# Attention's rough scores: one 128-row contraction against three 64-row matmuls in the two halves of TensorE's array

## The chip, the cores and the metric

The kernel is one launch on one NeuronCore of a Trainium2 chip. The metric is device time in microseconds (us) of one execution. TensorE (PE in the rows) multiplies, its weight loads are recorded apart (PEld); VectorE is DVE, ScalarE is ACT, GpSimd is POOL. In a matmul the stationary operand is loaded into the array and the moving operand's columns stream past it; both lie on SBUF partitions, and the partitions are the rows of the array over which the contraction runs.

## The reference, cut to what matters

The model normalizes 1250 rows of 768 features, sends them through two graph attention layers, and then through a transformer layer: attention with 12 heads of width 64, and a mixture of 8 experts. The change touches the attention's scores alone:

```python
def _attention(x, Wqkv, Wproj):                     # x: [1, 1250, 768], H = 12, HD = 64
    qkv = (x @ Wqkv).reshape(B, T, 3, H, HD)
    q, k, v = (qkv[:, :, 0], qkv[:, :, 1], qkv[:, :, 2])
    scores = jnp.einsum('bqhd,bkhd->bhqk', q, k) * jnp.float32(HD) ** (-0.5)
    attn = jax.nn.softmax(scores, axis=-1)
    out = jnp.einsum('bhqk,bkhd->bqhd', attn, v).reshape(B, T, D)
    return out @ Wproj
```

The softmax needs for each query a number near the maximum of its scores, to be subtracted before the exponential. It cancels in the quotient, so it need not be exact.

## The kernel before, in words

All matmuls of the attention take float32r operands. Precision is kept by splitting: a rounded part ("hi") and what it lacks ("lo").

Two heads make a pair `p` (six pairs), `e` is 0 or 1 within it. For each head four tiles of 128 partitions and 1250 columns hold, with `r = 64 * e`:

- `qst[:, e]`: q_hi in rows `r` to `r+63`, q_lo in the other half. `split` steps 0 and 2 on DVE write them (L1057, L1063) from `raw`.
- `kst[:, e]`: k_hi in both halves. DVE writes half `r` (L1060, `split` step 1), ACT writes the other (`set_k`, L946).
- `q2[:, e]`: a copy of q_hi in half `r` (`set_q` on ACT, L951), and in the first row of the other half the negated maxima (`set_m` on ACT, L956 and L957).
- `k2[:, e]`: k_lo in half `r` (`split` step 3 on DVE, L1067), and a row of ones in the first row of the other half (POOL, L1533 and L1534).

So `kst` times `qst` (L843) gives k_hi q_hi + k_hi q_lo, and `k2` times `q2` (L845) adds k_lo q_hi and the maxima's row. Both contract over 128 rows.

Before a head's scores can be taken, its maxima are needed. `rough(p, e, t)` (L811) computes the scores of 125 queries against all 1250 keys as three matmuls over the full 128 rows, 512, 512 and 226 columns, into PSUM banks 0 to 2 (L822 to L824). `maximum` on DVE (L1072) reduces those 1250 columns to one column, and the next `rough` waits for it, since there is one set of three banks. After ten of them `maxima` (L832) turns the ten columns into a row, and `set_m` writes it into `q2`.

The order of work is written out by hand. A head has 25 units `j`. In each unit TensorE takes four score matmuls of 250 columns (`scores`, L843 and L845) and six matmuls of 250 columns for an earlier unit (`weighted`, L864 to L866), ACT takes two exponentials of 500 columns (L974, L976), and DVE or POOL subtracts them (L1035, two and three units in five). Into this the next head's preparation is put by unit numbers: `ROUGH_AT[e]` gives the units after which TensorE takes a `rough` and before which DVE takes a `maximum`; `SET_K_AT`, `SET_Q_AT` and `SET_M_AT` give the units after which ACT writes `kst`, `q2` and the maxima. In head (p, 0) the preparation of (p, 1) is done, in head (p, 1) that of (p+1, 0). Between the two heads `project` (L793) computes q and k of the next pair, 108 matmuls of 416 or 418 columns, and ACT evicts them into `raw` (L939).

The first head's roughs stand before the pairs, between halves of the value projection (L912 to L915, `v_half`), with `set_q(0, 0)` on ACT after one more eviction of values (L1019, L1020). Each engine takes its instructions in the order in which they are written. Of the tuples above the first number belongs to the preparation of e = 1 and the second to that of e = 0.

Of the kernel before, what the change touches and what calls it, by code (L numbers as in the profile page):

```python
# [6 lines left out]
N = 1250  # L7
P = 125
# [95 lines left out]
def build(nc, x, src, dst, gw1, gas1, gad1, gb1, gw2, gas2, gad2, gb2,  # L104
# [123 lines left out]
    qst = put("qst", [128, 2, N], f32r, at=HEADS)  # L228
# [94 lines left out]
    with ctx:  # L323
# [3 lines left out]
        def sem(name):  # L327
            if name not in sems:
                sems[name] = ctx.enter_context(nc.semaphore(name))
            return sems[name]  # L330
# [435 lines left out]
        NUM_AT = ((8, 13, 18, 22), (9, 13, 18, 22))  # L766
        O_HI_AT, O_LO_AT = (18, 21), (20, 24)
        LAST_AT = ((10, 14, 20), (1, 5))
        SPLIT_AT, SET_K_AT, SET_Q_AT, SPLIT_QK_AT, LOWER_QK_AT = 2, (0, 3), 7, 9, (12, 14)

        def place(e, j):

# [16 lines left out]
        def attention_pe(pe):  # L789
# [21 lines left out]
            def rough(p, e, t):  # L811

                if t == 0:
                    pe.wait_ge(sem("q_lo"), 2 * p + e + 1)
                    pe.wait_ge(sem("k_hi"), 2 * p + e + 1)
                    pe.wait_ge(sem("kst_set"), 2 * p + e + 1)
                    pe.wait_ge(sem("raw_set"), 6 * p + 6)
                    if e == 1:
                        pe.wait_ge(sem("m_set"), 4 * p + 2)
                else:  # L820
                    pe.wait_ge(sem("max"), 20 * p + 10 * e + t)
                for c, (a, b) in enumerate(((0, 512), (512, 1024), (1024, N))):  # L822
                    last = pe.matmul(bank(c, P, b - a), qst[:, e, t * P:(t + 1) * P],  # L823
                                     kst[:, e, a:b], start=True, stop=True)  # L824
                last.then_inc(sem("rough"), 1)

            def maxima(p, e):
# [94 lines left out]
        def attention_act(act):  # L922
            def split_qk(p):
                act.wait_ge(sem("wq_in"), 32 * p + 32)

                if not isinstance(p, int) or p > 0:
                    act.wait_ge(sem("qk_raw"), 6 * p)
                act.activation(wqhi[:, :, :, :].rearrange("p m k c -> p (m k c)"),
                               wqst[:, :, :, :].rearrange("p m k c -> p (m k c)"), ACT.Copy).then_inc(sem("wq_hi"), 1)

            def set_raw(p, chunks=range(6)):

                if (not isinstance(p, int) or p > 0) and chunks[0] == 0:
                    act.wait_ge(sem("qk_split"), 2 * p)
                for j in chunks:
                    m, c = j // 3, j % 3
                    at, n = CHUNKS[c]
                    act.wait_ge(sem("qk_raw"), 6 * p + (j + 1))
                    act.activation(raw[:, m, at:at + n], bank(c, 128, n), ACT.Copy).then_inc(sem("raw_set"), 1)  # L939

            def set_k(p, e):

                r = 64 * e
                act.wait_ge(sem("raw_set"), 6 * p + 6)
                act.wait_ge(sem("q_hi"), 2 * p + e + 1)
                act.activation(kst[64 - r:128 - r, e, :], raw[r:r + 64, 1, :], ACT.Copy).then_inc(sem("kst_set"), 1)  # L946

            def set_q(p, e):

                r = 64 * e  # L950
                act.activation(q2[r:r + 64, e, :], qst[r:r + 64, e, :].bitcast(f32), ACT.Copy).then_inc(sem("q2_set"), 1)  # L951

            def set_m(p, e):
                r = 64 * (1 - e)
                act.wait_ge(sem("m_raw"), 2 * p + e + 1)
                act.activation(halves(q2[r:r + 1, e, 0:1000]), two(0, 1, 500), ACT.Copy).then_inc(sem("m_set"), 1)  # L956
                act.activation(q2[r:r + 1, e, 1000:N], bank(2, 1, 250), ACT.Copy).then_inc(sem("m_set"), 1)  # L957

            def numerators(p, e, g):

                act.wait_ge(sem("pv"), PAIR * p + (UNITS * e + 5 * g + 5 + PV0))
                if e == g == 0:
                    act.wait_ge(sem("v_set"), 2 * p + 2)
                b = (6 + (NG * e + g) % 2) * BANK
                act.activation(outt[64 * e:64 * e + HD, ds(p, 1), g * GQ:(g + 1) * GQ].rearrange("c o q -> c (o q)"),
                               ps[0:HD, b:b + GQ], ACT.Copy).then_inc(sem("o_part"), 1)

            def exps(p, e, between):

                for j in range(UNITS):  # L970
                    n = UNITS * e + j
                    act.wait_ge(sem("st"), PAIR * p + (n + 1))
                    act.wait_ge(sem("pv"), PAIR * p + (n + 1 + PV0 - RING))
                    act.activation(prhi[:, n % RING, :], bank(3 + n % 3, P, 2 * GQ), ACT.Exp, scale=float(HD) ** -0.5)  # L974
                    wait_lo(act, p, e, j - place(e, j)[1])
                    act.activation(prob[:, n % 3, :], bank(3 + n % 3, P, 2 * GQ), ACT.Exp, scale=float(HD) ** -0.5)\  # L976
                        .then_inc(sem("exp"), 1)
                    if j in between:
                        between[j]()

            def pair(p, last):
                steps = {SET_K_AT[0]: lambda: set_k(p, 1), SET_Q_AT: lambda: set_q(p, 1), SET_M_AT[0]: lambda: set_m(p, 1)}
                more = {}
                if not last:
                    steps[SPLIT_QK_AT] = lambda: split_qk(p + 1)
                    more = {LAG - 1: lambda: set_raw(p + 1, (5,)), SET_K_AT[1]: lambda: set_k(p + 1, 0),
                            SET_Q_AT: lambda: set_q(p + 1, 0), SET_M_AT[1]: lambda: set_m(p + 1, 0)}
                else:
                    for k in range(KD):
                        (steps, more)[k // 3][5 * (k % 3) + 9] = lambda k=k: split_act(act, 3, wpst, wphi, (k,))  # L990
                for g, j in enumerate(NUM_AT[0]):
                    steps[j] = lambda g=g: numerators(p, 0, g)
                if not isinstance(p, int) or p > 0:
                    steps[4] = lambda: numerators(p - 1, 1, NG - 1)
                exps(p, 0, steps)
                if not last:
                    for g, j in enumerate(NUM_AT[1]):
                        more[j] = lambda g=g: numerators(p, 1, g)
                    set_raw(p + 1, (0,))
                    numerators(p, 0, NG - 1)  # L1000
                    set_raw(p + 1, range(1, 5))
                else:
                    more[4] = lambda: numerators(p, 0, NG - 1)
                    for t in range(2):
                        more[O_HI_AT[t]] = lambda t=t: o_hi(act, t)
                exps(p, 1, more)

            act.sem_inc(sem("exp"), 3)
            act.sem_inc(sem("o_part"), 2)
            for t in range(T // 2 - 1):  # L1010
                if t:
                    v_higher(act, 2 * t + 2)
                v_higher(act, 2 * t + 3)
                v_out(act, t)
                if t == 1:
                    split_qk(0)
            set_raw(0)
            set_k(0, 0)
            v_out(act, T // 2 - 1)  # L1019
            set_q(0, 0)  # L1020
            for t in range(T // 2, T):
                v_out(act, t)
            set_m(0, 0)
            pair(0, False)
            with act.Fori(0, H // 2 - 2) as i:
                pair(i + 1, False)
            pair(H // 2 - 1, True)
# [16 lines left out]
        def attention_dve(dve, order):  # L1044
# [4 lines left out]
            def split(p, e, step):  # L1049
# [8 lines left out]
                elif step == 1:  # L1058
                    dve.wait_ge(sem("raw_set"), 6 * p + 6)
                    dve.tensor_copy(kst[r:r + 64, e, :], raw[r:r + 64, 1, :]).then_inc(sem("k_hi"), 1)  # L1060
                elif step == 2:
                    dve.wait_ge(sem("q_hi"), 2 * p + e + 1)
                    dve.tensor_tensor(qst[64 - r:128 - r, e, :], raw[r:r + 64, 0, :], qst[r:r + 64, e, :].bitcast(f32),  # L1063
                                      ALU.subtract).then_inc(sem("q_lo"), 1)
                else:
                    dve.wait_ge(sem("k_hi"), 2 * p + e + 1)
                    dve.tensor_tensor(k2[r:r + 64, e, :], raw[r:r + 64, 1, :], kst[r:r + 64, e, :].bitcast(f32),  # L1067
                                      ALU.subtract).then_inc(sem("qk_split"), 1)

            def maximum(p, e, t):  # L1070
# [402 lines left out]
        def _(pool):  # L1473
# [56 lines left out]
            pool.wait_ge(sem("v_row"), T)  # L1530
            order.did(pool.memset(k2[:, :, :].bitcast(f32), 0.0))
            order.wait()
            order.did(pool.memset(k2[64:65, 0, :].bitcast(f32), 1.0))  # L1533
            order.did(pool.memset(k2[0:1, 1, :].bitcast(f32), 1.0))  # L1534
            order.wait()
            pool.sem_inc(sem("set_pool"), 1)
            pool.wait_ge(sem("tile_y"), 3 * T + 2)
# [983 lines left out]
```

## Time and profile before

| | |
|---|---|
| time, median of 3 runs | 1533.46 us (1529.39 to 1536.1) |
| span of the profiled execution, first to last instruction | 1528.7 us |
| mean granted TensorE clock | 0.970 of 2.4 GHz |
| TensorE busy, matmuls | 1412.6 us (92%), 8981 |
| TensorE busy, weight loads | 1337.2 us (87%), 8981 |
| VectorE busy | 1154.8 us (76%) |
| ScalarE busy | 970.2 us (63%) |
| GpSimd busy | 493.7 us (32%) |
| rough matmuls (L823) | 360, from 598.8 to 1164.2 us |

The profile is one execution. The median of the runs is 4.8 us above its span; that is what lies around the span, and the spread between the runs. A busy share counts a matmul from its start to the modelled end of its results; such intervals overlap, so the time that a matmul costs TensorE is read from the start of one to the start of the next.

### The profile page before, as it was taken

The numbers are of one execution on the slowest core, as the hardware profiler recorded it, in microseconds if no ns is written. First come the engines' busy times: TensorE is split into PE (matmuls) and PEld (weight loads), VectorE is DVE, ScalarE is ACT, GpSimd is POOL, SyncE is SP. The second block draws the span as 40 slices with busy tenths as digits, with TensorE's granted clock in tenths as the row PEclk, the third lists the DMA queues.
The fourth block names the chain that finished last, engine by engine and source line by source line (L and its number), as shares of the span: only waits on it lengthen the run. The fifth ranks groups of instructions, "written<-read, shape, count | busy, mean of one in ns | idle before, by whom it ended". The sixth has DMA issues, their size and how long they took to land.

```text
span 1528.7 us, 25668 instructions
## 1 busy us (share of the span) xinstructions
PE 1412.6 (92%) x8981; PEld 1337.2 (87%) x8981; DVE 1154.8 (76%) x1756; ACT 970.2 (63%) x1658; POOL 493.7 (32%) x366
## 2 busy tenths in 40 slices
PE   3898799999799999999999999999999998699996
PEld 1897577999699999899898998999988898599996
DVE  6788979735689762486877868778788787888885
ACT  7997787522368431366848767478587522599995
POOL 2000000000000010244625536256356501288886
PEclk9999799999899999999999999999999998799999
DMA  7001000122214540000000000000001496476752
GB/s 202 1 1 36 6 14 18 52 100 73 102 54 131 182 142 22 1 21 1 1 21 0 21 0 0 21 0 0 21 1 32 121 296 165 126 155 162 164 94 36
DMA packets 52312, 99.09 MB, mean 65 GB/s; under 512 B 10848, under 2 KB 26852, under 8 KB 52224
## 3 DMA queue, kind: packets, MB, share of 16 engines
q1 hardware_dynamic: 40848, 75.68, 15.9%
q0 software_dynamic: 11376, 22.29, 7.5%
q8 instruction: 49, 0.80, 0.2%
q14 instruction: 39, 0.32, 0.1%
HBM read 67.15 MB, written 44.31 MB: 73 GB/s over the span
## 4 chain that ended last, share of the span: by engine, by line
PE 68%; DVE 9%; issue 3%; DMA 1%; ACT 1%; POOL 1%; POOLq 0%; ACTq 0%; DVEq 0%; SPq 0%
PE ps L372 14%; PE ps L373 14%; PE ps L374 14%; PE ps L823 4%; PE ps L864 4%; PE ps L843 3%; PE ps L866 3%; PE ps L845 3%; PE ps L865 3%; DVE mcol L1072 2%; PE ps L1257 1%; PE ps L598 1%; DVE prlo L1035 1%; PE ps L832 1%; PE ps L1674 1%
## 5 line engine op out<-in xcount | busy, mean ns | idle before, releaser
L1035 POOL TENSOR_TENSOR prlo<-prob,prhi 125x500 fp32r<-125x500 f32 x180 | 251.8, 1404 | 267.9 <-ACT prob L976 266.9
L1072 DVE TENSOR_REDUCE mcol<-ps 125x1 f32<-125x1250 f32 x120 | 174.9, 1458 | 73.0 <-PE ps L823 72.5
L974 ACT ACTIVATE prhi<-ps 125x500 fp32r<-125x500 f32 x300 | 176.8, 589 | 71.4 <-PE ps L845 65.4
L864 PE MATMUL ps<-prhi,vhi 125*128 125x250 f32 x600 | 172.5, 287 | 8.0 <-POOL prlo L1035 3.8
L976 ACT ACTIVATE prob<-ps 125x500 f32<-125x500 f32 x300 | 176.4, 588 | 0.6 <-DVE prlo L1035 0.6
L1529 POOL MEMSET q<- 128x2500 f32 x1 | 2.2, 2187 | 528.4 <-PE ps L374 528.4
L866 PE MATMUL ps<-prlo,vhi 125*128 125x250 f32 x600 | 168.8, 281 | 0.0
L865 PE MATMUL ps<-prhi,vlo 125*64 125x250 f32 x600 | 167.8, 280 | 0.0
L1674 PE MATMUL ps<-ohs,ohd 128*125 128x417 bf16 x380 | 126.0, 384 | 39.9 <-DVE ohs L2110 37.1
L843 PE MATMUL ps<-qst,kst 128*125 128x250 f32 x600 | 156.3, 284 | 3.5 <-ACT q L957 1.4
L372 PE MATMUL ps<-hhi,pthi 125*125 125x384 f32 x400 | 153.7, 384 | 3.0 <-DVE ptlo L712 3.0
L845 PE MATMUL ps<-q,k 128*125 128x250 f32 x600 | 153.5, 280 | 0.0
L1035 DVE TENSOR_TENSOR prlo<-prob,prhi 125x500 fp32r<-125x500 f32 x120 | 108.9, 908 | 46.3 <-ACT prob L976 45.3
L373 PE MATMUL ps<-hhi,ptlo 125*125 125x384 f32 x400 | 136.6, 341 | 0.0
L374 PE MATMUL ps<-hlo,pthi 125*125 125x384 f32 x400 | 135.9, 340 | 0.0
L864 PEld LDWEIGHTS ps<-prhi,vhi 125*128 125x128 f32 x600 | 114.4, 191 | 13.9 <-issue 5.5
L2110 DVE TENSOR_SCALAR ohs<-iota,scol,sval 128x420 bf16<-128x420 f16 x380 | 124.3, 385 | 0.0
L843 PEld LDWEIGHTS ps<-qst,kst 128*125 128x125 f32 x600 | 112.5, 188 | 10.6 <-issue 3.8
L1802 ACT ACTIVATE ohd<-iota,drel 128x125 bf16<-128x125 f16 x380 | 119.5, 390 | 0.3 <-POOLq L1502 0.3
L866 PEld LDWEIGHTS ps<-prlo,vhi 125*128 125x128 f32 x600 | 114.2, 190 | 0.0
L845 PEld LDWEIGHTS ps<-q,k 128*125 128x125 f32 x600 | 113.0, 188 | 0.0
L1674 PEld LDWEIGHTS ps<-ohs,ohd 128*125 128x125 bf16 x380 | 54.3, 144 | 65.8 <-DVE ohs L2110 47.2
(330 smaller groups left out, 4026.9 us busy)
## 6 DMA issues: line engine op xcount, KB each, us to landing
w1all<-in_L_ffn_W_dram SPq DMA_DIRECT2D x8, 1152.0 KB, 8.4
w2st<-in_L_ffn_W_dram SPq DMA_DIRECT2D x8, 1152.0 KB, 6.4
wqst<-in_L_ffn_Wqkv_dram SPq DMA_DIRECT2D x12, 384.0 KB, 4.2
hid_d<-tin SPq DMA_DIRECT2D x10, 375.0 KB
hin<-hid_d SPq DMA_DIRECT2D x10, 375.0 KB
vtin<-xn_d SPq DMA_DIRECT2D x10, 375.0 KB
out_dram<-accr POOLq DMA_DIRECT2D x10, 375.0 KB, 8.4
xall<-in_x_dram SPq DMA_DIRECT2D x5, 672.0 KB
```

Of the source, the lines that this page charges most:

```text
L372: pe.matmul(o, lhi, rhi, start=start, stop=False)
L373: pe.matmul(o, llo, rhi, start=False, stop=False)
L374: return pe.matmul(o, lhi, rlo, start=False, stop=stop)
L843: pe.matmul(o, kst[:, e, kt * P:(kt + 1) * P], qst[:, e, g * GQ:(g + 1) * GQ], start=True, stop=False)
L845: last = pe.matmul(o, k2[:, e, kt * P:(kt + 1) * P], q2[:, e, g * GQ:(g + 1) * GQ], start=False, stop=True)
L864: pe.matmul(ps[:, b:b + GQ], vhi[:, e, kt, :], hi, start=kt == 0, stop=False)
L865: pe.matmul(ps[0:HD, b:b + GQ], vlo[:, e, kt, :], hi, start=False, stop=False)
L866: last = pe.matmul(ps[:, b:b + GQ], vhi[:, e, kt, :], lo, start=False, stop=kt == T - 1)
L974: act.activation(prhi[:, n % RING, :], bank(3 + n % 3, P, 2 * GQ), ACT.Exp, scale=float(HD) ** -0.5)
L1035: eng.tensor_tensor(prlo[:, n % RING, :], prob[:, n % 3, :], prhi[:, n % RING, :].bitcast(f32), ALU.subtract)\
L1072: dve.tensor_reduce(mcol[:, e, t:t + 1], ps[0:P, 0:N], AX.X, ALU.max, negate=True).then_inc(sem("max"), 1)
L1674: pe.matmul(into, hots(b)[:, i, :], ohs[:, g % OHS, 0:PACK], start=u == 0, stop=u == WINDOW - 1).then_inc(sem("oh_free"), 1)
```

## The change

`rough` multiplies q_hi and k_hi alone, over 64 rows. Its three matmuls take different halves of the array: columns 0 to 511 and 1024 to 1249 in the half in which `qst` holds q_hi, columns 512 to 1023 in the other half, where `kst` holds its second k_hi. For that the copy of q_hi in `q2` moves to the other half, and with it k_lo in `k2`; the maxima's row and the ones change to the half left free. `rough` waits for q_hi and for the copy (`q2_set`) and no longer for q_lo. `set_q` waits for `q_hi` and is called after unit 1 or 4 where it was after unit 7; for the first head it is called one eviction earlier.

```diff
-        SPLIT_AT, SET_K_AT, SET_Q_AT, SPLIT_QK_AT, LOWER_QK_AT = 2, (0, 3), 7, 9, (12, 14)
+        SPLIT_AT, SET_K_AT, SET_Q_AT, SPLIT_QK_AT, LOWER_QK_AT = 2, (0, 3), (1, 4), 9, (12, 14)
+        ROUGH_PARTS = ((0, 0, 512), (1, 512, 1024), (0, 1024, N))
@@ rough
-                    pe.wait_ge(sem("q_lo"), 2 * p + e + 1)
+                    pe.wait_ge(sem("q_hi"), 2 * p + e + 1)
+                    pe.wait_ge(sem("q2_set"), 2 * p + e + 1)
@@
-                for c, (a, b) in enumerate(((0, 512), (512, 1024), (1024, N))):
-                    last = pe.matmul(bank(c, P, b - a), qst[:, e, t * P:(t + 1) * P],
-                                     kst[:, e, a:b], start=True, stop=True)
+                for other, a, b in ROUGH_PARTS:
+                    r = 64 * (1 - e if other else e)
+                    last = pe.matmul(ps[0:P, a:b], (q2 if other else qst)[r:r + 64, e, t * P:(t + 1) * P],
+                                     kst[r:r + 64, e, a:b], start=True, stop=True)
@@ set_q
-                act.activation(q2[r:r + 64, e, :], qst[r:r + 64, e, :].bitcast(f32), ACT.Copy).then_inc(sem("q2_set"), 1)
+                act.wait_ge(sem("q_hi"), 2 * p + e + 1)
+                act.activation(q2[64 - r:128 - r, e, :], qst[r:r + 64, e, :].bitcast(f32), ACT.Copy).then_inc(sem("q2_set"), 1)
@@ set_m
-                r = 64 * (1 - e)
+                r = 64 * e
@@ pair (ACT)
-                steps = {SET_K_AT[0]: lambda: set_k(p, 1), SET_Q_AT: lambda: set_q(p, 1), SET_M_AT[0]: lambda: set_m(p, 1)}
+                steps = {SET_K_AT[0]: lambda: set_k(p, 1), SET_Q_AT[0]: lambda: set_q(p, 1), SET_M_AT[0]: lambda: set_m(p, 1)}
@@
-                            SET_Q_AT: lambda: set_q(p + 1, 0), SET_M_AT[1]: lambda: set_m(p + 1, 0)}
+                            SET_Q_AT[1]: lambda: set_q(p + 1, 0), SET_M_AT[1]: lambda: set_m(p + 1, 0)}
@@ before the first pair (ACT)
             set_k(0, 0)
+            set_q(0, 0)
             v_out(act, T // 2 - 1)
-            set_q(0, 0)
@@ split, step 3
-                    dve.tensor_tensor(k2[r:r + 64, e, :], raw[r:r + 64, 1, :], kst[r:r + 64, e, :].bitcast(f32),
+                    dve.tensor_tensor(k2[64 - r:128 - r, e, :], raw[r:r + 64, 1, :], kst[r:r + 64, e, :].bitcast(f32),
@@ POOL
-            order.did(pool.memset(k2[64:65, 0, :].bitcast(f32), 1.0))
-            order.did(pool.memset(k2[0:1, 1, :].bitcast(f32), 1.0))
+            order.did(pool.memset(k2[0:1, 0, :].bitcast(f32), 1.0))
+            order.did(pool.memset(k2[64:65, 1, :].bitcast(f32), 1.0))
```

## Rows read from the trace of the kernel before

**Rows 1.** The page: each engine's busy time, and the chain's engines.
```profile
PE 1412.6 (92%) x8981; PEld 1337.2 (87%) x8981; DVE 1154.8 (76%) x1756; ACT 970.2 (63%) x1658; POOL 493.7 (32%) x366
...
PE 68%; DVE 9%; issue 3%; DMA 1%; ACT 1%; POOL 1%; POOLq 0%; ACTq 0%; DVEq 0%; SPq 0%
```

**Rows 2.** Timeline of PE (start us, us, engine, line): end of project, four units, one rough.
```profile
699.83 0.35 PE L374 MATMUL ps<-xtlo,wqhi 128*128 128x416 f32 x1
...
702.11 0.35 PE L374 MATMUL ps<-xtlo,wqhi 128*128 128x416 f32 x1
702.30 0.28 PE L843 MATMUL ps<-qst,kst 128*125 128x250 f32 x1
...
706.73 0.28 PE L865 MATMUL ps<-prhi,vlo 125*64 125x250 f32 x1
706.85 0.28 PE L866 MATMUL ps<-prlo,vhi 125*128 125x250 f32 x1
706.97 0.73 PE L823 MATMUL ps<-kst,qst 128*125 128x512 f32 x3
707.54 0.29 PE L843 MATMUL ps<-qst,kst 128*125 128x250 f32 x1
```

**Rows 3.** Timeline of PE at 1227 us: matmuls of 16 and 8 columns, back to back.
```profile
1227.07 0.25 PE L1225 MATMUL ps<-wrhl,ythi 128*125 128x16 f32 x1
...
1228.05 0.25 PE L1226 MATMUL ps<-wrhl,ytlo 128*125 128x8 f32 x1
```

**Rows 4.** Timeline at 709 us, PE and its weight loads: a restart after a wait.
```profile
709.08 0.27 PE L845 MATMUL ps<-q,k 128*125 128x250 f32 x1
...
709.28 0.19 PEld L864 LDWEIGHTS ps<-prhi,vhi 125*128 125x128 f32 x1
...
709.50 0.28 PE L865 MATMUL ps<-prhi,vlo 125*64 125x250 f32 x1
```

**Rows 5.** Timeline of ACT, head (1, 1): set_k, exponentials, and set_q.
```profile
801.71 1.25 ACT L946 ACTIVATE kst<-raw 64x1250 fp32r<-64x1250 f32 x1
...
803.47 0.58 ACT L976 ACTIVATE prob<-ps 125x500 f32<-125x500 f32 x1
...
807.08 1.25 ACT L951 ACTIVATE q<-qst 64x1250 fp32r<-64x1250 f32 x1
```

**Rows 6.** Timeline of PE, same head: its first rough.
```profile
804.54 0.73 PE L823 MATMUL ps<-kst,qst 128*125 128x512 f32 x3
```

**Rows 7.** Timeline of DVE, head (1, 0): maxima and what stands between them.
```profile
750.40 1.45 DVE L1072 TENSOR_REDUCE mcol<-ps 125x1 f32<-125x1250 f32 x1
...
761.64 1.57 DVE L1040 TENSOR_TENSOR wqlo<-wqst,wqhi 128x768 fp32r<-128x768 f32 x1
763.25 1.46 DVE L1072 TENSOR_REDUCE mcol<-ps 125x1 f32<-125x1250 f32 x1
```

**Rows 8.** Timeline of PE, same head: two of its roughs.
```profile
752.23 0.75 PE L823 MATMUL ps<-kst,qst 128*125 128x512 f32 x3
...
764.76 0.85 PE L823 MATMUL ps<-kst,qst 128*125 128x512 f32 x3 [0.35 <-DVE mcol L1072]
```

**Rows 9.** Busy time by engine: heads (1, 0) and (5, 0).
```profile
core 0: us, PE busy (x) PEld busy (x) DVE busy (x) ACT busy (x) POOL busy (x), PEclk, DMA share, GB/s
...
737.40:774.00 36.60, 35.45 (x274) 33.51 (x275) 31.84 (x28) 30.34 (x58) 24.85 (x17) 1.00 0.08 22
...
1130.00:1167.00 37.00, 33.86 (x258) 31.49 (x257) 35.70 (x32) 29.39 (x57) 28.66 (x20) 1.00 0.08 23
```

**Rows 10.** Timeline of all engines at the first rough, before the pairs.
```profile
596.38 1.25 ACT L946 ACTIVATE kst<-raw 64x1250 fp32r<-64x1250 f32 x1
...
597.22 1.46 DVE L1063 TENSOR_TENSOR qst<-raw,qst 64x1250 fp32r<-64x1250 f32 x1
598.71 1.45 DVE L1067 TENSOR_TENSOR k<-raw,kst 64x1250 fp32r<-64x1250 f32 x1
...
598.78 0.78 PE L823 MATMUL ps<-kst,qst 128*125 128x512 f32 x3
```

## The prediction

> **What bounds the kernel now.** I read the page first: TensorE is busy for 92% of the span, and 68% of the chain that ended last is TensorE's own [rows 1]. A busy share says little for matmuls that overlap, so I went on to the timeline of one head of attention and read the distance from one start to the next [rows 2]. From 699.83 to 702.11 there are 12 matmuls of 416 columns, 0.190 us each. From 702.30 to 706.97 there are 40 matmuls of 250 columns, 0.117 us each. Nothing stands between them: TensorE has work from start to start and is the bound here, at the full granted clock (1.00, 2.4 GHz) [rows 9]. Between the two sizes lie 0.073 us for 166 columns, 0.44 ns a column, which leaves 0.007 us for the matmul itself. A rough takes from 706.97 to 707.54, 0.57 us [rows 2]. The same two figures give it 0.232 + 0.232 + 0.107 = 0.571, for 512, 512 and 226 columns. So the price of columns is well known, and 120 roughs cost TensorE 68 us.
>
> Then the busy time by engine, to see who comes next. In head (1, 0) DVE is busy for 31.8 of 36.6 us, in the last pair's head (5, 0) for 35.7 of 37.0 [rows 9]. DVE takes each rough's maximum, and the next rough waits for it. In (5, 0) DVE and not TensorE sets the pace.
>
> **The change, part by part.** *The rough itself.* Let the first matmul (A, 512 columns) start at 0 in one half of the array. The second (B, 512, other half) has weights of its own to load. What a load of 125 columns costs when nothing hides it I take from matmuls with so few columns that only their loads are left: nine intervals from 1227.07 to 1228.05, 0.109 us each [rows 3]. B starts at 0.11 and its columns end at 0.34. The third (C, 226) needs A's half: from 0.232 to 0.339. Its weights load beside A and B. The next full matmul starts at 0.34 where it started at 0.571. So a rough gives back one matmul of 512 columns, 0.232 us, and 120 of them 27.8 us. This holds if the halves run beside each other and the array changes between one tile and two for nothing; no row here shows a 64-row matmul, so the cost of a rough is bounded from both sides: 0.34 at best, 0.57 if the halves take turns, and above that if changing over costs something (priced below). I take 0.34.
>
> What speaks for the free change is the nearest row. L865 has a stationary operand of 64 columns, 125*64, between two of 128. It starts 0.12 after L864 and 0.12 before L866, as all others do [rows 2], and there are 600 of these. A matmul that uses half the array's columns between matmuls that use all costs nothing. It is the other dimension, so it is a hint and no proof.
>
> The Trainium skill (TensorEngine Tiling (Array Packing), Key Properties) says that changing the tiling mode, not just the tile, drains the engine. If the 64-column matmul is such a mode, this case's rows disagree for columns, 0.12 us on either side; no run here yet shows rows. The Trainium skill (TensorE: Matmul & The Clock Gate, Part 3) says that matmuls in different row groups run at the same time; by that the sum is as above, by the first rule it is the rival below.
>
> *The copy of q_hi, earlier.* The rough now waits for `set_q`, 1.25 us on ACT [rows 5], where it waited for q_lo. q_lo was no gain to lose: inside the pairs DVE writes k_hi after it, and the rough still waits for k_hi.
> In heads (p, 1) the copy now stands behind the exponentials of unit 4. In head (1, 1) these end at 803.47 + 0.58 = 804.05, so the copy ends at about 805.35, and the rough that started at 804.54 [rows 6] starts at about 805.4, 0.85 late. Queued behind it on TensorE are the scores and weighted sums of units 7 and on, which wait too. ACT's exponentials 5 to 7 come 1.25 us later, and where the copy was (807.08) they have caught up. Short waits of TensorE for exponentials and their differences in the units behind it swallow some of that, I assume 0.15: 0.7 a pair, 3.5 us for five. The bounds are 0 (other stalls swallow it) and 1.25, 0 to 6 us in all.
> In heads (p, 0) the copy stands behind unit 1 and the rough behind unit 3. Two units of ten matmuls, 2.3 us, lie between, and the copy takes 1.25; exponential 2 comes 1.25 us later, which TensorE's lead of three units over its use covers. I take 0; without that cover it would be up to 1.25 a head.
> Before the pairs, `set_k` ends at 597.63 and the copy at about 598.9, where the rough started at 598.78 [rows 10]: 0.15 us once. The eviction behind it has two matmul groups of slack.
>
> *Where DVE takes back what TensorE gives.* In head (1, 0) the rough of 752.23 follows a maximum that ended at 751.85, 0.38 us before [rows 7, 8]. Three roughs gain 0.70 by then, so 0.3 is lost. The rough of 764.76 waits for a maximum that started at 763.25, behind `wqlo` (1.57 us): there DVE is in arrears since the rough two before, and one more 0.23 is lost. Together 0.55 a head in five heads, 2.8 us. In (5, 0) DVE has 1.3 us of idle left [rows 9]; I give it 1.0 of the 2.3. Elsewhere, as where two roughs stand in adjacent units, the wait for the maximum moves with the rough, which ends earlier itself, and nothing is lost.
>
> *Edits with one answer.* k_lo now crosses halves as q_lo did: 1.46 us crossing, 1.45 not [rows 10]. The copy crosses as `set_k` does, 1.25 both [rows 5]. The maxima's row and the ones are one partition each in either half. Adding q_lo k_hi no longer to the rough changes a number that cancels in the quotient. No DMA is moved.
>
> **The sum**, against the profiled span of 1528.7 us. Before the pairs 2.3 - 0.15 = 2.2. Heads (p, 0), five: 5 x (2.32 - 0.55) = 8.9. Heads (p, 1), five: 5 x (2.32 - 0.7) = 8.1. Head (5, 0): 1.0. Together 20.2 us, which gives a span of 1508.5. The median of the runs is 4.8 above the span, so 1513.
>
> **Rivals.**
> 1. *Changing over costs more than the columns give back.* Two changes a rough: into halves and out of them. If each waits until the results before it are out, it adds 0.28 - 0.117 = 0.163 us [rows 2]. If the weights can only be loaded after that, the load is no longer hidden: in a restart the load starts at 709.28 and the second next matmul at 709.50, 0.22 where 0.117 is the rule, 0.10 more [rows 4]. So 0.33 to 0.53 a rough against 0.232: 0.09 to 0.30 lost, 11 to 36 us, and the copy's 3.7 on top: 1548 to 1573. It decides from 0.085 us a change, since 20.2 / 120 = 0.17 is what two may cost. For it: the rule above. Against it: the 600 matmuls of L865. If this is so, the starts of L823 and of the L843 behind it are far apart.
> 2. *The halves take turns.* Then a rough costs 0.57 as before, and the copy's 3.7 us are all that is left: 1537. For it: nothing in this trace runs two matmuls at once. It is also how the change would fail to do what it says.
> 3. *Half a gain.* C starts only when B is done, 0.109 + 0.232 + 0.107 = 0.448 a rough: 0.123 x 120 = 14.8, less 3.7, less some 1 for DVE: 10 us, 1523. Or the halves run as hoped and DVE's arrears take all of the heads (p, 0): 1513 + 9 = 1522. For it: DVE's 87% in (1, 0). Against: its idle time there stands right before maxima, where it waits for the rough.
>
> **How the numbers follow.** The forecast 0.55, the third rival 0.15, the second 0.13, the first 0.17. A difference of over 0.5%, 7.7 us, is what a measurement of this kernel can tell from none. Faster by more: 0.55 and three quarters of 0.15, 0.66. Slower by more: the first rival less a little for small prices, 0.16. The rest 0.18. The range goes from 1504, all 27.8 us with a low run, to 1541, the turn-taking with the copy's dearer bound; it leaves out the first rival.
>
> **What would show it.** In the profile after, a rough's first start and the next L843's stand 0.34 us apart and B's start lies 0.11 behind A's (right), 0.57 (second rival), 0.45 with C late (third), or over 0.6 (first). The first rough of each head (p, 1) waits for ACT's copy by some 0.8 us, those of the heads (p, 0) don't. Waits for `mcol` grow in heads (p, 0) by half a microsecond each. The forecast is wrong if the spacing of roughs to their neighbours is off, since all else together is 8 us.

## The result, and the profile after

The changed kernel takes 1545.9 us (median of 4 runs, 1541.5 to 1547.4) against 1532.8 in the same comparison: ratio 1.0076, 95% interval 1.0058 to 1.0093. It is slower by 0.8%, where 1513 was forecast. The ratios of the experiments below are taken against runs of the kernel before made beside them (medians 1534.0 to 1534.5 us); one of those, at 2793.6 us, is left out of them.

| | before | after |
|---|---|---|
| span of the profiled execution | 1528.7 us | 1545.7 us |
| TensorE busy, matmuls | 1412.6 us (92%) | 1423.1 us (92%) |
| weight loads | 1337.2 us (87%) | 1317.3 us (85%) |
| VectorE busy | 1154.8 us (76%) | 1147.3 us (74%) |
| from the value projection to the last maxima | 639.0 us | 650.6 us |
| from there to the end | 361.9 us | 367.7 us |

The page of the changed kernel, busy times and the chain's engines, which answer to [rows 1]:

```profile
PE 1423.1 (92%) x8981; PEld 1317.3 (85%) x8981; DVE 1147.3 (74%) x1756; ACT 971.7 (63%) x1658; POOL 502.9 (33%) x366
...
PE 66%; DVE 6%; issue 4%; POOL 3%; ACT 2%; DMA 2%; ACTq 0%; POOLq 0%; SPq 0%; DVEq 0%
```

TensorE's loads are busy 20 us less and its matmuls 10.5 us more, though the change takes work away from it. 11.6 us of the 17 lie in the attention. I don't put the 5.8 behind it down to the change: the stretch from the last maxima to the end took 361.9 and 365.9 us in two traces of the kernel before, and between 362.0 and 368.5 in the twelve others, in no order that follows the edits (362.0 in `twice`, which has the most 64-row matmuls, and 368.5 in before_spread, which has none).

To see one rough, I take the stretch before the pairs, where it stands between matmuls of the value projection and waits for nothing. First the kernel before, timeline of PE:

```profile
621.09 0.34 PE L374 MATMUL ps<-wvlo,xthi 128*125 128x384 f32 x1
621.27 0.76 PE L823 MATMUL ps<-kst,qst 128*125 128x512 f32 x3
621.87 0.35 PE L372 MATMUL ps<-wvhi,xthi 128*125 128x384 f32 x1
622.05 0.33 PE L373 MATMUL ps<-wvhi,xtlo 128*125 128x384 f32 x1
```

Then the changed kernel, PE and below it its weight loads (the rough is L826):

```profile
621.98 0.34 PE L374 MATMUL ps<-wvlo,xthi 128*125 128x384 f32 x1
622.25 0.49 PE L826 MATMUL ps<-kst,qst 64*125 64x512 f32 x1
622.25 0.50 PE L826 MATMUL ps<-kst,q 64*125 64x512 f32 x1
622.58 0.26 PE L826 MATMUL ps<-kst,qst 64*125 64x226 f32 x1
622.78 0.44 PE L372 MATMUL ps<-wvhi,xthi 128*125 128x384 f32 x1
623.05 0.34 PE L373 MATMUL ps<-wvhi,xtlo 128*125 128x384 f32 x1
```

```profile
621.81 0.18 PEld L374 LDWEIGHTS ps<-wvlo,xthi 128*125 128x125 f32 x1
622.25 0.18 PEld L826 LDWEIGHTS ps<-kst,qst 64*125 64x125 f32 x1 [0.26 <-issue]
622.25 0.18 PEld L826 LDWEIGHTS ps<-kst,q 64*125 64x125 f32 x1
622.35 0.18 PEld L826 LDWEIGHTS ps<-kst,qst 64*125 64x125 f32 x1
622.77 0.18 PEld L372 LDWEIGHTS ps<-wvhi,xthi 128*125 128x125 f32 x1 [0.24 <-issue]
622.88 0.19 PEld L373 LDWEIGHTS ps<-wvhi,xtlo 128*125 128x125 f32 x1
```

From L374 to L373 it was 0.96 us, and 0.92 at other roughs of this stretch; now it is 1.07. The two 512-column matmuls start at the same moment, weight loads too, so the halves do run beside each other. But look at the loads. Where TensorE isn't held up, a load starts when the matmul before its own starts: that of L374 at 621.81, with L373's matmul. The first of the rough starts only 0.27 after L374, and that of L372 0.19 after the last of the rough. Each time nothing hides it. The next load (622.35, 622.88) shows when its weights were in place: 0.10 to 0.11 later. So the array stands still twice: out of whole rows into halves, and back.

The first rough of head (1, 1), ACT and PE, answers to [rows 5, 6]:

```profile
809.53 0.28 PE L869 MATMUL ps<-prlo,vhi 125*128 125x250 f32 x1
809.54 1.25 ACT L955 ACTIVATE q<-qst 64x1250 fp32r<-64x1250 f32 x1
...
809.88 0.28 PE L869 MATMUL ps<-prlo,vhi 125*128 125x250 f32 x1
810.98 0.49 PE L826 MATMUL ps<-kst,qst 64*125 64x512 f32 x1 [0.82 <-issue]
```

TensorE waits for the copy until 810.8. So there are two suspects, the change of rows and the copy's place, and the table that takes them apart is that of the heads' lengths, from the maxima of one to the maxima of the next. Pairs 1 to 4 agree to 0.1 us within each kernel, so one number stands for each:

| kernel (each is described below) | rough | copy after unit (e=1, e=0) | head (p, 0) | head (p, 1) with project | value projection to last maxima |
|---|---|---|---|---|---|
| before, two traces | 128 rows | 7, 7 | 38.9 | 58.8 | 639.0, 638.9 |
| after | halves | 1, 4 | 39.1 | 60.1 | 650.6 |
| full128 | 128 rows | 1, 4, waited for | 39.9 | 59.9 | 650.5 |
| full_q14 | 128 rows | 1, 4 | 40.1 | 59.9 | 650.9 |
| full_q74 | 128 rows | 7, 4 | 40.0 | 59.9 | 650.9 |
| full_q77 | 128 rows | 7, 7 | 40.0 | 58.8 | 644.1 |
| full_q77_lower10 | 128 rows | 7, 7 | 38.5 | 58.8 | 637.2 |
| copy_earlier | halves | 1, 3 | 39.0 | 60.3 | 649.7 |
| after_later | halves | 1, 5 | 39.1 | 60.6 | 650.8 |
| onehalf | one half only | 7, 7 | 41.0 | 61.2 | 669.2 |
| twice | halves, twice | 1, 4 | 42.1 | 63.2 | 686.1 |
| four_changes | half, whole, half | 1, 4 | 44.8 | 65.9 | 717.0 |
| before_spread | 128 rows | 7, 7 | 38.8 | 58.2 | 635.7 |

### The profile page after: what moved, and what is told of

Same layout as the page of the kernel before. It is cut to its first block, busy times and chain, and to the rows that moved or that the text cites. A ratio compares the mean times of both kernels' runs of the same rounds, so it can differ in the third digit from the quotient of the medians.

```text
span 1545.7 us, 25679 instructions
## 1 busy us (share of the span) xinstructions
PE 1423.1 (92%) x8981; PEld 1317.3 (85%) x8981; DVE 1147.3 (74%) x1756; ACT 971.7 (63%) x1658; POOL 502.9 (33%) x366
## 4 chain that ended last, share of the span: by engine, by line
PE 66%; DVE 6%; issue 4%; POOL 3%; ACT 2%; DMA 2%; ACTq 0%; POOLq 0%; SPq 0%; DVEq 0%
PE ps L372 13%; PE ps L373 13%; PE ps L374 12%; PE ps L846 5%; PE ps L826 4%; PE ps L867 4%; PE ps L869 3%; PE ps L868 3%; PE ps L848 3%; DVE mcol L1076 2%; PE ps L598 1%; PE ps L835 1%; PE ps L1261 1%; DMA xg<-xg_d,index 1%; POOL out_dram L1600 1%
## 5 line engine op out<-in xcount | busy, mean ns | idle before, releaser
L1039 POOL TENSOR_TENSOR prlo<-prob,prhi 125x500 fp32r<-125x500 f32 x180 | 246.3, 1372 | 280.8 <-ACT prob L980 280.3
L846 PE MATMUL ps<-qst,kst 128*125 128x250 f32 x600 | 166.7, 301 | 3.5 <-issue 1.4
L372 PE MATMUL ps<-hhi,pthi 125*125 125x384 f32 x400 | 153.4, 383 | 3.0 <-DVE ptlo L712 3.0
L1039 DVE TENSOR_TENSOR prlo<-prob,prhi 125x500 fp32r<-125x500 f32 x120 | 100.8, 841 | 50.8 <-ACT prob L980 50.3
L373 PE MATMUL ps<-hhi,ptlo 125*125 125x384 f32 x400 | 136.5, 341 | 0.0
L374 PE MATMUL ps<-hlo,pthi 125*125 125x384 f32 x400 | 135.9, 340 | 0.0
L1678 PEld LDWEIGHTS ps<-ohs,ohd 128*125 128x125 bf16 x380 | 54.2, 144 | 65.9 <-DVE ohs L2114 47.2
```

What stands on the lines that cost most here:

```text
L372: pe.matmul(o, lhi, rhi, start=start, stop=False)
L373: pe.matmul(o, llo, rhi, start=False, stop=False)
L374: return pe.matmul(o, lhi, rlo, start=False, stop=stop)
L846: pe.matmul(o, kst[:, e, kt * P:(kt + 1) * P], qst[:, e, g * GQ:(g + 1) * GQ], start=True, stop=False)
L1039: eng.tensor_tensor(prlo[:, n % RING, :], prob[:, n % 3, :], prhi[:, n % RING, :].bitcast(f32), ALU.subtract)\
L1678: pe.matmul(into, hots(b)[:, i, :], ohs[:, g % OHS, 0:PACK], start=u == 0, stop=u == WINDOW - 1).then_inc(sem("oh_free"), 1)
```

## The experiments

Two theories stood at the start. D: each change between whole rows and half rows costs TensorE about 0.19 us, twice a rough. W: the loss is the earlier copy of q_hi and the waits that it makes.

**full128**: the changed kernel with the rough of before.

```diff
+                    pe.wait_ge(sem("q_lo"), 2 * p + e + 1)
-                for other, a, b in ROUGH_PARTS: ...
+                for c, (a, b) in enumerate(((0, 512), (512, 1024), (1024, N))):
+                    last = pe.matmul(bank(c, P, b - a), qst[:, e, t * P:(t + 1) * P], kst[:, e, a:b], ...)
```

> The changed kernel with its rough made of three matmuls over 128 rows again, as before; it waits for the copy of q_hi and for q_lo. So all of the schedule of the change is left and only the 64-row matmuls are gone. Theory D (each change between full rows and half rows costs about 0.18 us, two per rough): the loss goes almost wholly, 1532 to 1537 us, at most 0.3% above the kernel before, and the first rough of five heads still waits some 0.8 us. Theory W (the earlier copy and its wait are the loss): about 1545 us, as the changed kernel.

Measured: 1546.2 us, ratio 1.0082 (1.0055 to 1.0108), as slow as the changed kernel. D alone had said 1532 to 1537. So the new schedule loses as much with whole roughs as the changed kernel loses with halves, and D doesn't explain this kernel. What that loss is took five more runs, below; they also show that it isn't made of the same parts in the two kernels, so that the equal times are partly chance.

**onehalf**: the kernel before, the rough in one half.

```diff
+                r = 64 * e
+                for a, b in ((0, 512), (512, 1024), (1024, N)):
+                    last = pe.matmul(ps[0:P, a:b], qst[r:r + 64, e, t * P:(t + 1) * P], kst[r:r + 64, e, a:b], ...)
```

> The kernel before, with the rough's three matmuls over the 64 rows of one half only, one behind the other; schedule and layout are those of before. Theory D: the changes between full and half rows stand alone with nothing gained beside them, 0.36 to 0.39 us a rough; times 120 is 43 to 47 us, less what TensorE's waits for DVE swallow, some 5 to 15: 1560 to 1575 us, and the distance from the last matmul before a rough to the second behind it grows from 0.82 to about 1.2 us. Theory W: 64 rows in one half stream as 128 do, no change, 1533 us.

Measured: 1565.1 us, ratio 1.0204 (1.0174 to 1.0235). The schedule is untouched, so this is the 64-row matmuls alone: the changes of rows, or a slower stream within the half, which `twice` below rules out. Timeline of PE:

```profile
619.62 0.34 PE L374 MATMUL ps<-wvlo,xthi 128*125 128x384 f32 x1
619.89 0.82 PE L824 MATMUL ps<-kst,qst 64*125 64x512 f32 x3
620.64 0.44 PE L372 MATMUL ps<-wvhi,xthi 128*125 128x384 f32 x1
620.92 0.34 PE L373 MATMUL ps<-wvhi,xtlo 128*125 128x384 f32 x1
```

1.30 us where 0.92 was: 0.38 for two changes. Times 120 this is 46 us; the kernel loses 31, since the heads have waits that swallow a part (2.2 and 2.4 us a head where ten roughs bring 3.8).

**four_changes**: half, whole, half.

```diff
+                for (rows, part), (a, b) in zip(((64 * e, qst), (None, qst), (64 * (1 - e), q2)),
+                                                ((0, 512), (1024, N), (512, 1024))):
+                    h = slice(0, 128) if rows is None else slice(rows, rows + 64)
+                    last = pe.matmul(ps[0:P, a:b], part[h, e, t * P:(t + 1) * P], kst[h, e, a:b], ...)
```

> The changed kernel with the rough's matmuls in another order: 512 columns in one half, 226 columns over all 128 rows, 512 columns in the other half. Four changes a rough instead of two, and no two halves beside each other. Theory D: 0.571 us of columns plus four changes of 0.18 to 0.20, so 0.36 to 0.40 for the two more and 0.232 for the overlap lost: 0.95 becomes 1.54 to 1.58 us; 120 x 0.6 = 72 us less what waits for DVE swallow, 1595 to 1618 us. If a cost stands at a rough once, whatever the changes within it: 0.95 becomes 1.18, 1565 to 1573 us.

Measured: 1614.4 us, ratio 1.0528 (1.0501 to 1.0555). Timeline of PE:

```profile
620.77 0.34 PE L374 MATMUL ps<-wvlo,xthi 128*125 128x384 f32 x1
621.04 0.79 PE L828 MATMUL ps<-kst,qst 64*125 64x512 f32 x2
621.76 0.49 PE L828 MATMUL ps<-kst,q 64*125 64x512 f32 x1
622.18 0.44 PE L372 MATMUL ps<-wvhi,xthi 128*125 128x384 f32 x1
622.46 0.34 PE L373 MATMUL ps<-wvhi,xtlo 128*125 128x384 f32 x1
```

1.69 us, 0.77 more than 0.92, for four changes: 0.19 each, as in onehalf, and the time is in the range expected. The price goes with the number of changes and isn't a price of the rough.

**twice**: `for other, a, b in 2 * ROUGH_PARTS`.

> The changed kernel with each rough computed twice in a row, six 64-row matmuls, nothing else. It measures what the same columns cost once the array is in halves. Theory D with full overlap: the second three add 0.232 + 0.107 = 0.34 us and no further change, 0.95 becomes 1.29 from the last matmul before to the second behind; 120 x 0.34 = 41 us, less waits for DVE: 1575 to 1587 us. Theory S (the halves slow each other, so that 512 beside 512 columns take 0.34 and not 0.232): the second three add 0.45 us, 54 us, up to 1600.

Measured: 1578.8 us, ratio 1.0301 (1.0275 to 1.0328). Timeline of PE:

```profile
618.91 0.34 PE L374 MATMUL ps<-wvlo,xthi 128*125 128x384 f32 x1
619.18 0.49 PE L826 MATMUL ps<-kst,qst 64*125 64x512 f32 x1
619.18 0.49 PE L826 MATMUL ps<-kst,q 64*125 64x512 f32 x1
619.51 0.26 PE L826 MATMUL ps<-kst,qst 64*125 64x226 f32 x1
619.52 0.39 PE L826 MATMUL ps<-kst,q 64*125 64x512 f32 x1
619.62 0.51 PE L826 MATMUL ps<-kst,qst 64*125 64x512 f32 x2
620.05 0.45 PE L372 MATMUL ps<-wvhi,xthi 128*125 128x384 f32 x1
620.34 0.34 PE L373 MATMUL ps<-wvhi,xtlo 128*125 128x384 f32 x1
```

1.43 against 1.07: the second three cost 0.36, where 0.34 was expected with full overlap and 0.45 with halves that slow each other. At 619.51 and 619.52 both halves take their next matmul, with no exposed load: within the halves all works as hoped.

**Where the copy stands.** Three kernels like full128 (whole rough, layout of the change), without the rough's wait for `q2_set` and with other places of the copy:

```diff
-        SPLIT_AT, SET_K_AT, SET_Q_AT, SPLIT_QK_AT, LOWER_QK_AT = 2, (0, 3), (1, 4), 9, (12, 14)
+        SPLIT_AT, SET_K_AT, SET_Q_AT, SPLIT_QK_AT, LOWER_QK_AT = 2, (0, 3), (7, 7), 9, (12, 14)   # full_q77
+        ... (7, 4) ...   # full_q74
+        ... (1, 4) ...   # full_q14
-                    pe.wait_ge(sem("q2_set"), 2 * p + e + 1)
```

> Rough over 128 rows as before, layout of the change (copy of q_hi, k_lo, maxima and ones in changed halves), copy of q_hi after unit 7 in both heads as before; the rough doesn't wait for it. Theory P (place: the loss of the kernel with 128-row roughs, some 11 us, comes from where ACT takes the copy): back to the kernel before, 1530 to 1537 us, period of a pair 97.7 us. Theory L (layout: k_lo written across halves, or the eviction moved before the pairs): still about 1545, period 99.9.

> Rough over 128 rows, copy after units 1 and 4 as in the change, but the rough doesn't wait for it. Theory P with the wait as its first half: TensorE's wait of 0.97 us at the first rough of five heads is gone, and the wait of 1.3 us for a maximum late in the heads (p, 0) stays: period 98.9 us, 1540 to 1542 us. If the wait for the copy was all: 1534; if place alone was all: 1545.

> As the last, with the copy for e = 1 back after unit 7 and that for e = 0 after unit 4, no wait for it. Only the heads (p, 1) are changed against the kernel before. Theory P, with its larger half in the heads (p, 0): no loss left beyond 1 to 2 us, 1532 to 1538, and no wait of 1.3 us for a maximum in the heads (p, 0). If the heads (p, 1) carry the loss by more than their wait: above 1540.

Measured: 1539.9 (1.0033, 1.0020 to 1.0047), 1544.6 (1.0079, 1.0055 to 1.0102) and 1545.8 us (1.0074, 1.0045 to 1.0102). The first missed both of its values: half of the loss stays with every copy at its old place. The other two missed the values of theory P and came where the other branch of their expectations stood: full_q14 at the 1545 of "place alone", full_q74 above 1540. The table sorts it out. Heads (p, 1) lose 1.1 us as soon as their copy stands after unit 4, whether the rough waits for it or not. Heads (p, 0) lose 1.1 to 1.2 us in full128 and in all three of these kernels, whatever the copy's place.

The 1.1 us first. Timeline of full_q74 in head (1, 1), POOL and PE:

```profile
810.62 1.25 POOL L1038 TENSOR_TENSOR prlo<-prob,prhi 125x500 fp32r<-125x500 f32 x1 [1.10 <-ACT prob L979]
...
812.11 0.35 PE L866 MATMUL ps<-prhi,vhi 125*128 125x250 f32 x1 [0.88 <-POOL prlo L1038]
```

No rough waits here. The copy holds back ACT's next exponential by 1.25 us, POOL subtracts it later, and the weighted sum on TensorE waits for POOL. `set_k`, also 1.25 us, has used up ACT's lead one unit before. Take one wait away and the next stands in its place.

**copy_earlier** tried the other way, in the changed kernel:

```diff
-        ... (0, 3), (1, 4), 9 ...
+        ... (0, 3), (1, 3), 9 ...
-                    more = {LAG - 1: lambda: set_raw(p + 1, (5,)), SET_K_AT[1]: lambda: set_k(p + 1, 0),
+                    more = {LAG - 1: lambda: (set_raw(p + 1, (5,)), set_k(p + 1, 0)),
```

> The changed kernel, 64-row roughs, with set_k for e = 0 right after unit 2 and the copy after unit 3 instead of 3 and 4. The copy ends about one unit (0.95 us) sooner, so the wait of 0.98 us at the first rough of five heads shrinks to under 0.1: 4 to 5 us less than the changed kernel, 1541 us. The changes between full and half rows stay, 0.19 us each. If the later exponentials (1.25 us earlier hit) cost as much at another place: 1545, no gain.

Measured: 1547.5 us, ratio 1.0096 (1.0066 to 1.0126); heads (p, 1) 60.3 us, no better than 60.1, as the second branch of the expectation had it. In head (1, 1) the first rough starts 0.8 us sooner after the last maxima (31.1 for 31.9), and the second comes 4.45 us behind it instead of 3.46. Between the two a weighted sum now waits 0.70 us for POOL. The loss has moved one interval on.

**The collision.** Now the 1.15 us of the heads (p, 0). Timeline of full_q77 in head (1, 0): POOL, DVE, and the rough that waits:

```profile
757.81 1.31 POOL L1038 TENSOR_TENSOR prlo<-prob,prhi 125x500 fp32r<-125x500 f32 x1 [0.64 <-ACT prob L979]
757.91 2.02 DVE L1043 TENSOR_TENSOR wqlo<-wqst,wqhi 128x768 fp32r<-128x768 f32 x1
...
765.99 0.84 PE L825 MATMUL ps<-kst,qst 128*125 128x512 f32 x3 [1.30 <-DVE mcol L1075]
```

The same place in the kernel before:

```profile
757.89 0.95 DVE L1040 TENSOR_TENSOR wqlo<-wqst,wqhi 128x768 fp32r<-128x768 f32 x1
758.08 1.87 POOL L1035 TENSOR_TENSOR prlo<-prob,prhi 125x500 fp32r<-125x500 f32 x1 [0.65 <-ACT prob L976]
```

Whoever starts first takes about what it takes with no subtraction on the other engine (0.95 or 1.31 here; in full_q77_lower10, below, 0.94 and 1.27), and the other takes longer, 1.87 or 2.02. In the kernel before DVE is ahead by 0.19 us, in full_q77 POOL by 0.10. Over all traces this holds down to small distances: with POOL ahead by 0.05 us, in the first pair of onehalf, the step takes 2.03, and with DVE ahead by 0.01, in four_changes, 0.95. DVE is in arrears at this point, as [rows 7, 8] show, and 1.07 us more end in a wait of 1.3 us at the eighth rough. **full_q77_lower10** moves that step into DVE's idle time:

```diff
-        ... (7, 7), 9, (12, 14)
+        ... (7, 7), 9, (10, 14)
```

> The kernel full_q77 (rough over 128 rows, changed layout, old places of the copy) with one edit: DVE lowers the first half of the next pair's q and k weights after unit 10 instead of 12, where it was idle 0.99 us before a maximum. Theory C (collision: with POOL at its subtraction when DVE begins, that step takes 2.02 us instead of 0.95, the maxima behind it are late and TensorE waits 1.3 us for one of them): the step takes 0.95, the 1.16 us a head (p, 0) go, heads (p, 0) take 38.9 us or less, 1540 becomes 1534 or less. If the layout itself costs time in these heads: still 40.0.

Measured: 1533.4 us, ratio 0.9996 (0.9979 to 1.0012). Timeline of DVE:

```profile
752.56 0.94 DVE L1043 TENSOR_TENSOR wqlo<-wqst,wqhi 128x768 fp32r<-128x768 f32 x1
753.63 1.46 DVE L1075 TENSOR_REDUCE mcol<-ps 125x1 f32<-125x1250 f32 x1
```

The step takes 0.94, heads (p, 0) fall from 40.0 to 38.5, and the kernel is level with the one before. before_spread, with the old layout and the step at the same place, has 38.8 in these heads. So the changed layout, k_lo across halves and the evictions before the pairs, costs nothing of its own. What loses there is a hit between DVE and POOL that 0.3 us of timing turn on and off; what in the new layout moves POOL ahead by those 0.3 us is not shown.

In the changed kernel the hit is off in the pairs 1 to 4 (POOL starts 0.03 behind DVE, the step takes 0.95) and on in the first (2.02). In full128 it is on in all of them. So full128 loses 1.1 us in each head (p, 0) to the hit, the changed kernel 0.2 to its dearer roughs, and that both end at 1546 us is partly luck.

**after_later** put the copy and the roughs of the heads (p, 1) later in the changed kernel:

```diff
-        ROUGH_AT = (..., (6, 8, 10, 12, 14, 16, 17, 19, 21, 22))
+        ROUGH_AT = (..., (7, 9, 11, 13, 15, 17, 18, 20, 21, 22))
-        ... (1, 4), 9, (12, 14)
+        ... (1, 5), 9, (10, 14)
```

> The changed kernel, 64-row roughs, with that same edit, the copy for e = 0 after unit 5 and the roughs of the heads (p, 1) one unit later, three pairs of them in adjacent units instead of two. If ACT's arrears of 1.25 us behind set_k are what the heads (p, 1) lose, the first rough's wait of 0.98 falls to about 0.3 and the heads (p, 1) take 59.4 to 59.7 us instead of 60.1; heads (p, 0) keep 39.0. 1546 becomes 1543. Still over the kernel before: the changes between full and half rows stay.

Measured: 1545.2 us, ratio 1.0067 (1.0041 to 1.0093). Heads (p, 1) take 60.6 us, not 59.4 to 59.7. The first rough waits no longer. In head (1, 1) these waits stand in its place, PE:

```profile
808.46 0.38 PE L867 MATMUL ps<-prhi,vhi 125*128 125x250 f32 x1 [0.37 <-POOL prlo L1039]
...
813.23 0.49 PE L826 MATMUL ps<-kst,qst 64*125 64x512 f32 x1 [0.54 <-DVE mcol L1076]
```

The second is the second rough's. Two things were moved at once, the copy and the roughs (one more pair of them in adjacent units), so the run doesn't say what the copy alone costs after unit 5. After unit 7 it is free, in the kernels with whole roughs. Head (0, 0) took 40.5 us for 42.3: there the lowering step, now after unit 10, takes 0.94 and not 2.02.

**before_spread and before_again.** The runs show where the kernel before waits: at roughs in adjacent units (from the last matmul before such a rough to the second behind it 1.43 to 1.48 us, where 0.81 is the rule in a head), so

```diff
-        ROUGH_AT = (..., (6, 8, 10, 12, 14, 16, 17, 19, 21, 22))
+        ROUGH_AT = (..., (5, 7, 9, 11, 13, 15, 17, 19, 21, 22))
-        ... 7, 9, (12, 14)
+        ... 7, 9, (10, 14)
```

> The kernel before with two numbers moved and nothing of the change: the roughs of the heads (p, 1) after units 5, 7, 9, 11, 13, 15, 17, 19, 21, 22, so one adjacent pair instead of two, and DVE's lowering step after unit 10 instead of 12. A rough in a unit adjacent to the last waits 0.54 us for the maximum; one such wait in five heads is 2.7 us; the heads (p, 0) lose their wait of 0.35 at the eighth rough, 1.7 us. 1533 becomes 1529, ratio 0.997. If other waits take their place: no difference.

> The kernel before once more, for a second trace: heads (p, 0) 38.9 us and heads (p, 1) 58.8 us again, the lowering step 0.95 us; what comes after the last maxima 362 or 368 us, as it was 361 to 362 in four traces and 366 to 368 in the rest, whatever was changed in the attention.

Measured: 1530.3 us, ratio 0.9971 (0.9956 to 0.9987), some 4 us faster than the kernel before (2 to 7 by the interval) and the fastest of all. Heads (p, 1) fall by 0.6 us as expected. Heads (p, 0) don't: 38.8, their two long intervals stay. The second trace of the kernel before repeats 38.9 and 58.8 us and a step of 0.95 (0.94 in three of five). Its stretch behind the last maxima, 365.9 us, was neither of the two values expected, 362 and 368.

## Why the prediction was wrong

*The columns were right.* Three 64-row matmuls over two halves were to take 0.34 us, and `twice` gives 0.36. The way there was another: the second matmul doesn't start 0.11 behind the first, after a load of its own, but with it (622.25 twice). The 0.34 stand because the two matmuls in one half, 0.232 and 0.107, add up to the same. The halves overlap fully, weight loads among them. The rivals of halves that take turns (0.57) and of C behind B (0.45) fall.

*The step that failed: changing over for nothing.* "I take 0.34" rested on L865, a matmul over half the array's columns at 0.12 us to either side [rows 2], and called it a hint. It holds for columns and says nothing for rows: a change of rows costs 0.19 us, by onehalf and four_changes. It splits into about 0.08 to 0.10 of standing still and 0.11 for a load that nothing hides. So a rough costs 0.38 for two changes less 0.23 for the columns saved, 0.15 more than before, and not 0.23 less. The first rival had the step and bounds of 0.33 to 0.53 for two changes, which hold the 0.38; its break-even of 0.085 a change was passed twice over. Its parts were others: it let each change wait 0.163 us, until the results before it are out, and the measured wait is 0.08 to 0.10.

The Trainium skill (TensorEngine Tiling (Array Packing), Key Properties) says that a change of tiling mode drains the engine. That a change of rows costs time the traces bear out; that the engine is empty first they don't show, since the load at 622.25 starts 0.07 us before the modelled end of L374 (621.98 + 0.34). For columns the 0.12 us of L865 speak against the rule, if a stationary operand of 64 columns is such a mode.

*The copy.* 0.7 us a pair was a size off and its mechanism half right. The first rough does wait, 0.82 us, but it costs 1.1 a pair even where no rough waits for the copy (full_q74 against full_q77, 59.9 and 58.8). The cost is ACT's lead, used up by two steps of 1.25 us one unit apart. In heads (p, 0) I took 0 and that held but for the first, (0, 0), whose rough waits 0.66 us for it: full_q74 and full_q77 differ only in the place for (p, 1), full_q14 and full_q74 only in that for (p, 0), and the latter are both at 40.0 to 40.1. The 0.15 us before the pairs didn't come: the copy ends at 598.86 and TensorE's rough starts at 598.96 without a wait.

*DVE.* I had it take back 0.55 us a head of TensorE's gain. With roughs that got longer it did the reverse. In head (1, 0) the nine intervals between roughs were 3.32, 3.08, 2.91, 2.92, 3.30, 2.91, 3.40, 3.02 and 2.89 us, and are 3.39, 3.04, 3.07, 3.04, 3.07, 3.05, 3.11, 3.06 and 3.03. Four undisturbed ones grow by 0.12 to 0.16, the two in which TensorE stood in a wait shrink by 0.23 and 0.29; the sum grows by 0.1. In this way ten roughs of 0.15 add 0.2 us to a head (p, 0) instead of 1.5. The wait that I let grow at the eighth rough is gone (3.40 became 3.11). The roughs add 0.2 to a head (p, 1) too (60.1 for the 59.9 of full128), where the roughs in adjacent units come 2.15 us apart for 2.29, since the chain through the maximum has got shorter.

*The sum, with what was measured,* value projection to last maxima: before the pairs 1.8 us (roughs 0.15 dearer, 1.3, and 0.5 until the first rough, which the second trace of before has too), head (0, 0) 2.5 (the collision and a wait for the copy), four heads (p, 0) 0.9, five heads (p, 1) 6.4, head (5, 0) -0.1: 11.5 of the 11.6. By cause: the copy 5.5 (five times 1.1), dearer roughs 3.0, head (0, 0) 2.5, the late start 0.5. Against the forecast gain of 20.2 us, 31.8 are missing. 27 of these are the roughs, which were to bring 23.9 after DVE's share and cost 3.0; 2 are the copy, 2.5 head (0, 0), 0.5 the late start. The 13 us between the medians are this and the spread of the rest. Head (0, 0)'s 2.5 is from one trace of each; in the second trace of before that head is 0.5 shorter.

*Around the span* lie 1.7 us and not 4.8: the profiled execution of before was a short one among runs from 1527 to 1540.

What stays open: what the copy alone costs after unit 5, what in the new layout shifts DVE against POOL, and how much of the changed kernel's loss in the heads (p, 1) would be left at unit 7, where its roughs could not start before unit 8.

## What to carry to other kernels

Before using a half of TensorE's rows for a matmul between whole ones, count the changes: here 0.19 us each way against 0.44 ns for every column saved, so that one visit must save over 860 columns (0.38 / 0.44 ns), or hold many matmuls. What a matmul of half the array's columns cost (nothing) did not tell what half the rows cost. And where an engine's lead hides a step, move it only after asking what has used the same lead one unit before; taking the wait away moved the loss and didn't lower it.

## What the runs showed of the hardware

- Whole rows to half rows or back: 0.19 us, 0.08 to 0.10 of it before the next weight load starts and 0.11 the load (onehalf, four_changes; loads of 125 columns at the full granted clock). 128 to 64 columns: nothing (0.12 us on either side of L865).
- Two halves load weights and stream 512 columns each at the same time, and each goes on to its next matmul by itself (622.25 twice; 619.51 and 619.52).
- DVE's subtraction of 128 x 768 takes 0.95 us alone or first, 2.02 when POOL's subtraction of 125 x 500 has started 0.10 us before it; POOL's takes 1.31 in that case and 1.87 when DVE is first.
